# VectorE adds a shared group's rows ahead of the next expert rows in the last stage, and ScalarE's weight splits move behind the first expert rows' high parts

## What is computed

```python
h = gelu(x[:, 1:] @ W1 + x[:, :1] @ W2 + b)              # token projection, 255 rows a batch
h = h + attention(layernorm(h))                          # 16 heads of 64
xf = layernorm(h)                                        # rows of the mixture of experts
topw, topi = top_k(softmax(xf @ router_w), 2)            # two of 8 experts a row
routed = sum over the two experts of topw * (silu(xf @ w1[e]) @ w2[e])
gate, up = split(xf @ shared_gate_up)
shared = sigmoid(xf @ shared_gate_w) * ((silu(gate) * up) @ shared_down)
out = h + routed + shared
```

## Time and profile before

| | us |
|---|---|
| median of 3 runs | 1019.66 |
| lowest, highest run | 1019.19, 1021.77 |
| the profiled execution | 1021.38 |
| its span, first to last instruction | 1019.6 |
| mean granted TensorE clock in it, as a share of full speed | 0.996 |

### The profile page before, as it was taken

How to read it: one execution, slowest core, us unless ns; L and a number is a source line. 1 busy time by engine, 2 the same in 40 slices (tenths; PEclk the granted TensorE clock), 3 DMA queues, 4 the chain that set the end, 5 groups by cost and what they waited for, 6 DMA issues and landing times.

```text
span 1019.6 us, 23069 instructions
## 1 busy us (share of the span) xinstructions
PE 998.7 (98%) x7994; PEld 867.1 (85%) x7994; DVE 735.9 (72%) x1912; ACT 651.9 (64%) x1924; POOL 527.9 (52%) x574
## 2 busy tenths in 40 slices
PE   9989999999999999999999999999999999999988
PEld 7878888888888888888898889888887889999977
DVE  4867785786788578857858885786677676766666
ACT  5678883775677477747846884786577465555421
POOL 0045633556456455735555564557245498555543
PEclk9999999999999999999999999999999999999999
DMA  9120000101100010100011000101104727666387
GB/s 309 43 49 1 2 2 1 43 1 44 42 1 23 22 42 2 43 22 22 7 39 42 1 27 17 43 1 44 42 1 172 248 91 217 194 206 183 116 279 232
DMA packets 42583, 74.30 MB, mean 73 GB/s; under 512 B 8183, under 2 KB 27415, under 8 KB 42471
## 3 DMA queue, kind: packets, MB, share of 16 engines
q1 hardware_dynamic: 33671, 47.62, 14.3%
q0 software_dynamic: 8496, 25.18, 7.6%
q10 hardware_dynamic: 304, 0.03, 0.0%
HBM read 40.28 MB, written 32.52 MB: 71 GB/s over the span
## 4 chain that ended last, share of the span: by engine, by line
PE 80%; DVE 7%; ACT 2%; DMA 2%; issue 2%; SPq 0%; POOL 0%; POOLq 0%; DVEq 0%; ACTq 0%
PE proj_ps L73 11%; PE proj_ps L75 11%; PE proj_ps L74 11%; PE pT_ps L817 11%; PE proj_ps L830 10%; PE s_ps L799 9%; PE s_ps L73 2%; PE s_ps L75 2%; PE s_ps L74 2%; PE proj_ps L1091 2%; PE proj_ps L1092 2%; PE proj_ps L1086 1%; PE s_ps L1046 1%; DMA back<-expert_out_rows 1%; PE pT_ps L1076 1%
## 5 line engine op out<-in xcount | busy, mean ns | idle before, releaser
L1142 ACT ACTIVATE prob<-s_ps,nmax 128x255 f32<-128x255 f32 x512 | 238.3, 480 | 137.9 <-DVE nmax L1352 137.0
L1862 POOL TENSOR_SCALAR prob<-prob,rinv 128x255 f32<-128x255 f32 x128 | 138.4, 1081 | 254.0 <-DVE rinv L1370 253.5
L1352 DVE TENSOR_REDUCE nmax<-s_ps 128x2 f32<-128x510 f32 x256 | 159.3, 680 | 22.4 <-PE s_ps L799 21.8
L817 PEld LDWEIGHTS pT_ps<-ident,prob 128*128 128x128 f32 x1024 | 114.8, 140 | 32.6 <-issue 24.2
L817 PE MATMUL pT_ps<-ident,prob 128*128 128x128 f32 x1024 | 136.5, 276 | 0.0
L830 PE MATMUL proj_ps<-probT,v 128*64 128x256 f32 x1024 | 124.9, 386 | 0.4 <-DVE probT L1377 0.4
L1864 POOL TENSOR_SCALAR prob<-prob,rinv 128x255 f32<-128x255 f32 x128 | 119.4, 933 | 0.0
L1359 DVE TENSOR_TENSOR qk_space<-proj_ps,qk_space 128x512 fp32r<-128x512 f32 x128 | 87.7, 685 | 33.4 <-ACT qk_space L1154 33.0
L1149 ACT ACTIVATE prob<-prob,rinv 128x255 f32<-128x255 f32 x128 | 67.1, 524 | 66.4 <-DVE rinv L1370 66.3
L799 PE MATMUL s_ps<-qk_space 64*128 64x256 f32 x1536 | 108.3, 287 | 0.4 <-DVE qk_space L1359 0.4
L1142 ACT ACTIVATION_READ_ACCUMULATOR prob<-s_ps,nmax 128x1 f32 x512 | 108.6, 212 | 0.0
(11 more groups left out here) (275 smaller groups left out, 2681.5 us busy)
## 6 DMA issues: line engine op xcount, KB each, us to landing
xg<-expert_in_rows SPq DMA_DIRECT2D x71, 130.0 KB
back<-expert_out_rows SPq DMA_DIRECT2D x6, 1024.0 KB, 15.8
xin<-in_x_dram SPq DMA_DIRECT2D x8, 512.0 KB, 4.6
z_columns<-z2T_hi SPq DMA_DIRECT2D x8, 512.0 KB, 2.6
z_columns<-z2T_lo SPq DMA_DIRECT2D x8, 512.0 KB, 3.7
out_dram<-resid SPq DMA_DIRECT2D x7, 448.0 KB
z3T_hi<-z_columns POOLq DMA_DIRECT2D x5, 512.0 KB, 5.0
z3T_lo<-z_columns POOLq DMA_DIRECT2D x5, 512.0 KB, 4.8
```

What stands on the lines that cost most here:

```text
L817: m = pe.transpose(pT_ps[h][:, o:o + P], prob[u_par(u)][:, h, qt, kt * P:(kt + 1) * P], ident[:])
L1142: m = act.activation(prob[u_par(u)][:, h, qt, 1:N], s_ps[b][h][:, qt * N + 1:(qt + 1) * N], ACT.Exp, bias=nmax[b][:, n:n + 1], accum_out=r ...
L1352: dve.tensor_reduce(nmax[b][:, 2 * h:2 * h + 2], s_ps[b][h][:].rearrange("p (q k) -> p q k", q=2)[:, :, 1:N], AX_X, ALU.max, negate=True). ...
L1862: pool.tensor_scalar(prob[k][:, 0, 1, 1:N], prob[k][:, 0, 1, 1:N], rinv[k][:, 1:2], None, ALU.mult).then_inc(s_nA1, 1)
```

## The change

No instruction is added or taken away; some move within ScalarE's and VectorE's queues. The order on TensorE, GpSimd and SP is untouched.

```diff
@@ ScalarE, ahead of the expert stage @@
             hidden_split_hi(1, 0)
             silu(1, 1)
             split_hi(1)
+            split_hi(2)
             hidden_split_hi(1, 1)
-            split_hi(2)
+            silu(2, 0)
             split_hi(3)
-            silu(2, 0)
-            split_hi(4)
             hidden_split_hi(2, 0)
             silu(2, 1)
...
             x_hi(0)
             hidden_split_hi(2, 1)
             x_hi(1)
+            split_hi(4)
             split_hi(5)
@@ VectorE, ahead of the expert stage @@
             hidden_split_lo(1, 0)
             hidden_split_lo(1, 1)
+            product(2, 0)
             add_shared(0)
-            product(2, 0)
-            hidden_split_lo(2, 0)
             product(2, 1)
...
             x_lo(0)
+            hidden_split_lo(2, 0)
             hidden_split_lo(2, 1)
             add_shared(1)
             x_lo(1)
@@ VectorE, behind the expert stage @@
             add_first(3)
             product(5, 0)
-            add_second(4)
             add_shared(3)
             product(5, 1)
+            add_second(4)
             add_first(4)
             add_shared(4)
```

## The result

| | before | after |
|---|---|---|
| median, us | 1020.71 (4 runs) | 1013.83 (4 runs) |
| lowest, highest run | 1019.19, 1023.44 | 1012.76, 1014.50 |
| the profiled execution | 1021.38 | 1014.0 |
| its span | 1019.6 | 1012.3 |
| its mean granted clock | 0.996 | 0.997 |

The ratio is 0.9931, with a 95% interval of 0.9914 to 0.9948: the kernel is 5.3 to 8.8 us faster. A second comparison, with 12 runs after and 35 before, gave 1013.82 against 1020.24, ratio 0.9946 (0.9929 to 0.9963), 3.8 to 7.2 us. (The ratio is not the quotient of the two medians: these lie 6.9 apart in the first comparison and 6.4 in the second.) The predicted 1014.5 was 0.7 from the median, and the forecast's direction and range held.

What follows compares the result with a forecast made beforehand. TensorE, busy 998.7 of 1019.6 us, was taken to bound the kernel. Gains of 4.35 behind and 1.22 ahead of the experts made 5.57, less 0.43 gave 5.1 off the median 1019.66: 1014.5 us, range 1013.0 to 1016.7.

Steps and rivals of the forecast that it cites:

- The head: Ahead of the experts: TensorE's gaps before up(0), 0.66, and shared_rows(2), 0.56, both go; 1.22 us won.
- The tail: Behind the experts: 3.09 of the gap before shared_rows(4) and 1.26 of low clock behind it won, 4.35 us.
- rest gap: Ahead of shared_rows(4): 0.12 us of the 3.21 gap was expected to be left.
- The discount of 0.43: Taken off the gain at the median: a fourth of the 1.72 us between profiled execution and median.
- Rival 2: Behind the experts: stall mostly the profiled execution's; that stretch wins only 1.2 us, total 1017.3; chance 0.10.
- Rival 1: Behind the experts: transfers take a part back, winning 3.1 instead of 4.35 us, total 1015.8; chance 0.23.
- Rival 3: Behind the experts: load 5 is overtaken and add_second(5) waits; 1023.5 us were loads held back by 12; chance 0.03.
- Rival 4: Both places: nothing moves, as something else keeps TensorE; 1019.7 us; chance 0.04.
- The loop: Expert loop: TensorE's 0.60 wait for a load may double or vanish, -0.6 to +0.6 us, taken as nothing.

Runs made afterwards that it cites:

- seven executions: Profiles with the old order behind the experts: four of the kernel before, three with only edits ahead of the experts; hidden(3) to hidden(6) 24.23 to 26.81 us.
- the moved add: Kernel after with add_second(4) one place further ahead, between add_shared(3) and product(5, 1): median 1014.99 us, ratio 0.9950.
- VectorE's half alone: Kernel before with only VectorE's moves ahead of the experts: hidden(2) to the experts' first transposes 14.82 us, against 14.62 before.
- third execution: Kernel before, unchanged, profiled a third time: gap ahead of shared_rows(4) 2.06 us, clock fell, hidden(3) to hidden(6) 25.84 us.
- the tail edit alone: Kernel before with only the edit behind the experts, add_shared(3) and product(5, 1) ahead of add_second(4): median 1017.71 us, ratio 0.9977.
- second execution of the kernel after: Kernel after, unchanged, profiled again beside the two halves: median 1013.82 us, ratio 0.9946.

## Why the prediction was right, and where it was not

**The mechanism held at both places.** Behind the experts the wait went for the reason given: an add that needs nothing of a load no longer stands behind one that does. Ahead of them `x_lo(0)` and `add_shared(1)` come earlier, at 819.33 and 820.92 in place of 821.85 and 823.24, since the products ahead of them no longer wait for ScalarE's weight copies and for `add_shared(0)`. The sequencer's work on line 1062 moved under `shared_rows(1)` (at 820.2, 1.1 ahead of `up(0)`), as said; whether it or `x_lo(0)` ended the old wait of `up(0)`, no run here separates.

**The head was sized 1.22 and measured 1.70.** The step that failed is reading a gap as what a gap costs. In the kernel before, the last two matmuls of `shared_rows(1)` and the second of `up(0)`, which began at 822.72:

```profile
821.68 0.28 PE L74 MATMUL proj_ps<-sd_lo,z2T_hi 128*128 128x256 f32 x1
821.79 0.28 PE L75 MATMUL proj_ps<-sd_hi,z2T_hi 128*128 128x256 f32 x1
...
822.94 0.29 PE L74 MATMUL s_ps<-up_lo,xgT_hi 128*128 x1
```

The profile counts idle time from the modelled end of a matmul, 0.28 behind its start, but at full pace the next one starts 0.12 behind it: each gap costs 0.16 more than its bracket says. And the first matmul behind one takes 0.20 to 0.22 to the next start in place of 0.12. I kept `up(0)` at 1.53 - 0.56 = 0.97, and it takes 0.72; `shared_rows(1)` at 2.98, and it takes 2.82. Two gaps: 2 x 0.16 + 0.09 + 0.07 = 0.48, which is the difference of 1.70 and 1.22.

**The tail was sized 4.35, measured 4.74 in the profiled pair, and is about 3.2 over seven executions, 3.5 with what falls behind the stage.** For the pair the errors are small: the same 0.16; the 0.12 of rest gap that didn't come, since VectorE lost the meeting with GpSimd at `add_second(2)` before (2.62) and won it after (1.22), and so came to `product(5, 0)` 1.1 us earlier; and 0.11 of `shared_rows(4)`, 2.87 in place of 2.98. Where VectorE lost it, with the moved add, 0.35 was left over, close to 0.12 + 0.16; so the new order, too, can have two lengths. For the median the term was too large, because one execution stood for all: it held the longest of seven stalls, and a clock fall that four of seven have. The theory had load 4's landing as what sizes the stall; in five of the seven GpSimd's subtraction did, as told above.

**The discount of 0.43** rested on the right suspicion, that the stall differs from run to run, and its size was a choice. By the runs it should have been 4.8 - 3.5 = 1.3 (both counted to the end), and the head should have been 0.5 more and the tail in the pair 0.4 more. 1.70 + 3.5 = 5.2 stands beside the 5.1 predicted: the number is right since the errors cancel, which is luck. The second comparison, 3.8 to 7.2, holds 5.2. The first, 5.3 to 8.8, begins a little above it, and the medians are 6.4 and 6.9 apart; I found no place in the changed stretches for the rest, and it stays open.

**Rival 2, the stall as an accident of the profile,** was half right: the size is the execution's. Its condition, load 4 in time, was not met in any: load 4 landed 0.59 to 1.55 behind the point at which VectorE asked for it in all seven, as the prediction argued from the full DMA engines. The smallest tail gain is 2.2 and not 1.2.

**Rival 1, transfers that take a part back:** its mechanism is there, and in the kernel after it cost nothing. Load 7 landed 4.8 later behind its issue, but VectorE asked for it some 3.4 behind its landing (973.7 + 25.5 = 999.2, against 1002.63). The accumulating transfers went out at 988.28 in place of 994.47, and the store of group 0, which waits for them, at 996.71 in place of 1001.95: 3.6 and 2.7 earlier, counted from `hidden(3)`. So their landings did move, and from `hidden(6)` to the end the two kernels take the same time. It can cost: with the moved add SP's last stores ran with VectorE long done, as this rival had it, for some 1.3 us.

**Rival 3** needed load 5 behind 998.92; `add_second(5)` ran at 991.68 without a wait. **Rival 4** is excluded by the ratios and by the gaps that are gone. The loop was costed at nothing between bounds of -0.6 and +0.6: its waits for expert rows are 0.42 and 0.23 now, 0.65 together (0.60 before).

## What to carry to other kernels

When an engine's order is written by hand, look for an instruction that feeds the bounding engine and stands behind one that waits for a load it doesn't need, and put it ahead; but ask of the instruction that you put ahead of it what that one waits for, since VectorE's half alone made the head slower. Take the cost of a gap from the starts on both sides of it at full pace, not from the idle time printed. And before a stall that hangs on a landing or on which of two engines comes first is priced, profile several executions: here the same code lost between 2.2 and 4.7 us in it.

## What the hardware showed

- **The granted clock after a short gap isn't decided by the gap's length alone.** Of gaps of 2.12 to 2.13 us with the same work around them two were followed by half clock and two were not; `shared_rows(4)` took 4.17 to 4.41 where it fell, against 2.87 to 2.95 where it didn't.
- **VectorE's two-input add and GpSimd's subtraction exclude each other**: at `add_second(4)` 1.22 to 1.23 against 1.56 to 2.12 for the add, 1.26 to 1.29 against 2.20 to 2.32 for the subtraction, by who starts first. A lead of 0.03 us (third execution) was enough to be the first, and being second cost VectorE up to 0.9.
- **The part that nobody touched moves by 4 us.** `shared_rows(1)` started at 821.13 in the run with the tail edit alone and at 816.98 in the second execution of the kernel after. Part of it is the clock, which fell in the former just ahead (a window with the columns of the earlier trace rows):

```profile
805.00:810.00 5.00, 4.74 (x25) 3.96 (x24) 2.39 (x8) 3.48 (x8) 4.05 (x4) 0.74 0.94 331
```

In the latter it is 1.00 there. The runs of before lie between 1015.75 and 1024.36, those of after between 1012.16 and 1015.07; why the runs of after lie so close together was not settled.
